# NF4 weight chunks worked out in turned layout, with block maxima from a second, natural copy

## The reference

```
x = x + attention(layernorm(x), ctx, ctx, mask; Wq, Wk, Wv, Wo)   # 32 query heads, 8 key/value heads of 128
x = x + ffn(layernorm(x); w1, w2, w3)

attention: q, k with rotary embedding; logits * 0.0884, 30*tanh(./30), masked softmax, times v, times Wo
ffn:       (silu(x @ dq(w1).T) * (x @ dq(w2).T)) @ dq(w3).T       # w1, w2: 1376 x 512, w3: 512 x 1376
dq(w):     flat = w.reshape(-1, 64); absmax = max|flat| per block of 64
           idx = searchsorted(bounds, flat / absmax); dq = NF4_CODE[idx] * absmax   # 16 levels, 15 bounds
```

## Time and profile before

| | |
|---|---|
| median of 3 runs | 800.41 us |
| profiled execution | 800.16 us |
| its span in the profile | 798.3 us |
| VectorE busy | 661.7 us, 83% of the span |
| ScalarE busy | 547.4 us, 69% |
| GpSimd busy | 367.3 us, 46% |
| moved by DMA | 87.56 MB, 110 GB/s on average |

### The profile page before, as it was taken

The page is one execution under the profiler, slowest core; times in us unless marked ns, Lnnn a source line. Parts: engine busy times, 40 slices in busy tenths (PEclk is TensorE's granted clock), DMA queues, the critical chain, the costliest instruction groups (busy, mean ns, idle before and its releaser), DMA issues.

```text
span 798.3 us, 10879 instructions
## 1 busy us (share of the span) xinstructions
PE 789.0 (99%) x3810; PEld 635.9 (80%) x3810; DVE 661.7 (83%) x741; ACT 547.4 (69%) x859; POOL 367.3 (46%) x210
## 2 busy tenths in 40 slices
PE   8999999999999999999999999999999999999998
PEld 6777887878887788878888888888778888888876
DVE  6897755898999999898988889899574999999913
ACT  6467737787877868678787788786643877868510
POOL 4773265446637457366465365473100534435010
PEclk9999999999999999999999999999999999999999
DMA  9636456333432433425235335231401031412022
GB/s 335 199 129 201 131 155 169 110 99 93 139 107 77 154 97 112 129 71 171 79 84 152 92 93 165 80 103 47 136 14 40 27 126 54 124 28 76 14 69 106
DMA packets 60981, 87.56 MB, mean 110 GB/s; under 512 B 6272, under 2 KB 29952, under 8 KB 60928
## 3 DMA queue, kind: packets, MB, share of 16 engines
q1 hardware_dynamic: 59744, 84.06, 35.7%
q10 hardware_dynamic: 1184, 2.82, 1.0%
HBM read 51.00 MB, written 19.07 MB: 88 GB/s over the span
## 4 chain that ended last, share of the span: by engine, by line
PE 85%; DVE 6%; issue 5%; ACT 2%; DMA 1%; POOL 0%; POOLq 0%; SPq 0%; DVEq 0%
PE bank L530 7%; PE prjs L514 7%; PE prjs L516 7%; PE bank L532 7%; PE bank L531 7%; PE prjs L515 7%; PE bank L590 7%; PE avp L618 6%; PE trp L503 4%; PE bank L496 3%; PE bank L498 3%; PE bank L497 3%; PE prjs L498 2%; PE prjs L496 2%; PE prjs L497 2%
## 5 line engine op out<-in xcount | busy, mean ns | idle before, releaser
L1294 POOL TENSOR_TENSOR qT<-cs_loop,sw 128x512 f32<-128x512 f32 x56 | 107.2, 1915 | 183.4 <-DMA sw<-cs_loop 176.1
L514 PE MATMUL prjs<-xh,wqh 128*128 128x512 f32 x256 | 123.3, 482 | 0.0
L530 PE MATMUL bank<-woh,ath 128*128 128x512 f32 x256 | 100.8, 394 | 1.0 <-DVE atl L1161 0.9
L516 PE MATMUL prjs<-xh,wql 128*128 128x512 f32 x256 | 100.2, 391 | 0.0
L532 PE MATMUL bank<-woh,atl 128*128 128x512 f32 x256 | 99.9, 390 | 0.0
L531 PE MATMUL bank<-wol,ath 128*128 128x512 f32 x256 | 99.7, 389 | 0.0
L862 ACT ACTIVATE ath<-trp 128x512 fp32r<-128x512 f32 x64 | 38.2, 596 | 89.5 <-PE trp L503 89.5
L515 PE MATMUL prjs<-xl,wqh 128*128 128x512 f32 x256 | 99.5, 389 | 0.0
L995 DVE TENSOR_TENSOR cs_loop<-prjs,csq 128x1024 f32<-128x1024 f32 x56 | 68.3, 1220 | 21.4 <-PE prjs L516 21.2
L987 DVE SCALAR_TENSOR_TENSOR nfv<-nfq,nfv 128x1408 f32<-128x1408 uint8 x42 | 79.1, 1883 | 0.2
L850 ACT ACTIVATE nrm<-avp,rs 128x128 f32<-128x128 f32 x256 | 72.6, 372 | 7.0 <-DVE rs L1148 6.7
(11 more groups left out here) (187 smaller groups left out, 1966.6 us busy)
## 6 DMA issues: line engine op xcount, KB each, us to landing
sw<-cs_loop SPq DMA_DIRECT2D x112, 128.0 KB, 2.3
stage<-wq_pieces SPq DMA_DIRECT2D x32, 256.0 KB, 2.9
stage<-wo_pieces SPq DMA_DIRECT2D x32, 256.0 KB, 3.1
stage<-dq_scratch SPq DMA_DIRECT2D x32, 256.0 KB, 3.2
ks_scratch<-qT SPq DMA_DIRECT2D x16, 256.0 KB, 3.1
vs_scratch<-vst SPq DMA_DIRECT2D x16, 256.0 KB, 3.5
kcur<-ks_scratch SPq DMA_DIRECT2D x16, 256.0 KB, 2.9
vcur<-vs_scratch SPq DMA_DIRECT2D x16, 256.0 KB, 3.4
```

The source lines that it names most:

```text
L514: nc.tensor.matmul(o, wqh[:, g, k, :], xh[:, k, cs], start=k == 0, stop=False)
L516: last = nc.tensor.matmul(o, wql[:, g, k, :], xh[:, k, cs], start=False, stop=k == KT - 1)
L530: nc.tensor.matmul(o, ah, wh[:, g, :], start=g == 0, stop=False)
L1294: nc.gpsimd.tensor_tensor(dst, products(ru, slot)[:, 0, :], sw[:, slot, :], ALU.add).then_inc(roped, 1)
```

## The change

The host now lays the chunks out turned: a partition holds a column of the contraction, so that the dequantised piece can be used as it lies, and the 64 values of a block lie in 64 (w1, w2) or 32 (w3, one of 4 parts) partitions. A second copy of the weights, `nf_natural`, in the old layout, is loaded as well, a chunk at a time (`nat_load`, buffer `nat`), for the maxima alone.

- `nf_top(k)` replaces `nf_prepare`: the same reduction and two small operations, on `nat`. For each k below 8 PE turns the 44 columns of maxima and reciprocals by one transpose (`turn_tops`), for w3 (k = 8 to 11 together) by two. ScalarE copies the rows out (`tops_rows`), SP stores them (`rows_store`: one transfer for k below 8, 32 small ones for w3).
- `scale_load(which, c)` loads them back, each row repeated over 64 or 32 partitions, into the one buffer `scl` (128 x 1408): two transfers for chunks 0 to 7, four for 8 to 11, before each normalising (which = 1) and each rescaling (which = 0).
- `nf_scale` replaces `nf_blocks`: both inputs are full 128 x 1408 tensors.
- All transposes of weights leave PE. `weight_hi`, `weight_lo`, `down_hi` and `w3_low` read `stage`, in SBUF; the loads of pieces wait for `wt_lo` in place of `wt_done`.
- The stream of items has all 12 maxima ahead: one per nine additions. 130 items (120 additions, 10 maxima) now lie in the loop, 34 in the hidden stage, 11 in the down stage. The maxima of chunk 0 move to VectorE's key unit 8 (turned on PE behind key unit 9), those of chunk 1 to value unit 10 (turned behind value unit 11).
- Chunks 0 to 7 are now those of w1 and w2, 8 to 11 those of w3. `nomask` and `keep` share the space of `eb`, and the scratch for dynamic DMA is set to 4096.

The diff, cut to its core:

```diff
+        SCALES = [(1, 0), (0, 0), (1, 1)] + ([x for c in range(2, 9) for x in ((1, c), (0, c - 1))]
+                                            + [(0, 8), (1, 9), (1, 10), (0, 9), (1, 11), (0, 10), (0, 11)])
+        ADDS = [(c, i) for c in range(1, 12) for i in range(15)]
+        STREAM = [x for n, add in enumerate(ADDS)
+                  for x in ([(n // 9 + 2, None)] if n % 9 == 0 and n < 90 else []) + [add]]
+        LOOP_ITEMS = STREAM.index((9, 0))
...
             if slot <= NSTEP:
-                return 122 * min(max(0, slot - 1), 55) // 55
+                return LOOP_ITEMS * min(max(0, slot - 1), 55) // 55
             if slot <= NSTEP + 2 * HT:
-                return 122 + 43 * min(max(slot - NSTEP - 2, 0), 20) // 20
-            return min(165 + max(0, 3 * (slot - NSTEP - 2 * HT) - 1), 16 * 11)
+                return LOOP_ITEMS + 34 * min(max(slot - NSTEP - 2, 0), 20) // 20
+            return min(LOOP_ITEMS + 34 + max(0, 3 * (slot - NSTEP - 2 * HT) - 1), len(STREAM))
...
+            def rows_store(k):
+                sp.wait_ge(rows_done, k + 1)
+                if k < 8:
+                    sp.dma_start(tops_d[k], rows[0:44, 0, :]).then_inc(rows_out, 16)
+                    return
+                for which in range(2):
+                    for part in range(4):
+                        to = tops3_d[which, part].rearrange("(n q a) r -> q a n r", q=2, a=2)
+                        for q, first in enumerate((part // 2, 21 + (part + 1) // 2)):
+                            for a in range(2):
+                                at = 44 * a + first
+                                sp.dma_start(to[q, a], rows[at:at + 21:2, which, :]).then_inc(rows_out, 16)
+            def scale_load(which, c):
...
+                    for half in range(2):
+                        at = 22 * which + 11 * half
+                        sp.dma_start(scl[64 * half:64 * half + 64, :],
+                                     tops_d[c, at:at + 11, :].rearrange("r h -> (r h)").partition_broadcast(64))\
+                            .then_inc(scale_in, 16)
...
+            def nf_transfers(slot):
+                for c in nf_norms(slot - 2):
+                    scale_load(0, c - 1)
+                for c in nf_finished(slot - 1):
+                    nf_store(c)
+                for c in nf_finished(slot - 2):
+                    if c < 7:
+                        nf_load(c + 2)
+                        scale_load(1, c + 2)
+                    if c == 7:
+                        scale_load(0, 8)
+                for k in nf_tops(slot - 2):
+                    if k < 8 or k == 11:
+                        rows_store(min(k, 8))
+                for k in nf_tops(slot - 1):
+                    if k < 11:
+                        nat_load(k + 1)
...
+            def turn_tops(k, j=0):
+                pe.wait_ge(nf_max, 3 * k + 3 if k < 8 else 36)
+                wait(pe, rows_done, k)
+                wait(pe, y_done, j)
...
-                    if last and b in (2, 3):
-                        weight_transposes(b - 2)
-                    if last and b == 5:
-                        weight_transposes(2)
+                    for k in tops_turned(j):
+                        turn_tops(k, j)
...
-                act.wait_ge(wt_done, n + 1)
+                if n == 0:
+                    act.wait_ge(roped, NK + NUNIT)
+                act.wait_ge(piece_in[n % 4], 16 * (STAGED + n // 4 + 1))
...
-                                     wt_bank(n)[:, :].rearrange("p (k h) -> p k h", k=KT), ACT.Copy).then_inc(wt_hi, 1)
+                                     stage[:, n % 4, :].rearrange("p (k h) -> p k h", k=KT), ACT.Copy).then_inc(wt_hi, 1)
...
-            def nf_blocks(buf, by):
-                blocks = buf[:, :].rearrange("p (b e) -> p b e", e=BLK)
-                return nc.gpsimd.tensor_tensor(blocks, blocks, by.rearrange("p (b o) -> p b o", o=1)
-                                               .to_broadcast([128, CH // BLK, BLK]), ALU.mult)
+            def nf_scale(buf):
+                return nc.gpsimd.tensor_tensor(buf[:, :], buf[:, :], scl[:, :], ALU.mult)
```

More of the change, by code:

```diff
@@ L74, in build @@
         nfp = sb("nfp", [128, 2, CH], u8)
-        nfm = sb("nfm", [128, 2, CH // BLK])
+        nat = sb("nat", [128, CH])
+        scl = sb("scl", [128, CH])
         nfg = sb("nfg", [128, CH // BLK])
-        nfr = sb("nfr", [128, CH // BLK])
+        tops = sb("tops", [128, 2, CH // BLK])
+        tops3 = sb("tops3", [128, 2, 4 * CH // BLK])
+        rows = sb("rows", [128, 2, 128])
         stage = sb("stage", [128, 4, 512])
@@ new lines, in scale_load @@
+            def scale_load(which, c):
+                if which == 0:
+                    if c in (8, 11):
+                        sp.wait_ge(nf_scaled, c)
+                    else:
+                        sp.wait_ge(nf_norm, c + 2 if c > 0 else 1)
+                else:
+                    wait(sp, nf_norm, c)
+                    wait(sp, nf_scaled, c if c in (1, 9) else c - 1)
+                if c < 8:
+                    sp.wait_ge(rows_out, 16 * (c + 1))
+                    for half in range(2):
[4 more added lines that the diff above has]
+                    return
+                sp.wait_ge(rows_out, 16 * 8 + 16 * 32)
+                for part in range(4):
+                    units = tops3_d[which, part, 11 * (c - 8):11 * (c - 7), :]
+                    sp.dma_start(scl[32 * part:32 * part + 32, :],
+                                 units.rearrange("u r -> (u r)").partition_broadcast(32)).then_inc(scale_in, 16)
@@ L543, in first_transposes @@
                 transpose4(trp, lambda k: nrm[:, i % 2, k * 128:(k + 1) * 128]).then_inc(xt_done, 1)
+            def turn_tops(k, j=0):
+                pe.wait_ge(nf_max, 3 * k + 3 if k < 8 else 36)
+                wait(pe, rows_done, k)
+                wait(pe, y_done, j)
+                out = tops_bank(k, j)
+                if k < 8:
+                    last = nc.tensor.transpose(out[0:44, 0:128], tops[:, :, :].rearrange("p w b -> p (w b)"), tab[:, 2, :])
+                else:
+                    for w in range(2):
+                        last = nc.tensor.transpose(out[0:88, w * 128:w * 128 + 128], tops3[:, w, :], tab[:, 2, :])
+                last.then_inc(nf_turned, 1)
             pe.wait_ge(consts, 2)
@@ L1378, in head @@
                         query_rope(j + AHEAD)
+                    if last and b == 3:
+                        nf_normalise(9)
                     if last and b in (2, 4, 6):
```

254 lines of the change are left out of this document (132 added, 122 removed).

## The result

The changed kernel takes 829.56 us (828.17 to 831.02 in 4 runs), the kernel before, run beside it, 800.48 us: 1.0363 times as long, interval 1.0343 to 1.0382. It is 29.1 us slower; the prediction said 8.0 us faster and at most 801. The profiled execution took 830.14 us with a span of 828.0 us.

The account below looks back on a forecast made before the run. PE, busy for 99% of the span, was taken to bound the kernel. The terms -15.3 + 1.5 + 2.1 - 0.6 + 3.0 + 0.5 + 0.8 = -8.0 us gave 792.4 us, range 786 to 801.

Parts of the forecast that it names:

- rival 3: SP's queue, blocked by 32 small stores of w3's maxima for 15.4 us: 0 to 5 us, 796 us; chance 0.13.
- Removed: Weight transposes leave PE: 22 groups at 0.46 us and 11 at 0.47 us, -15.3 us.
- Turnings: Nine turnings of maxima added on PE, 0.17 us each, +1.5 us.
- Start: Key projections: PE waits for first maxima, +2.1 us; chunk 1's maxima leave the place ahead of attention, -0.6 us.
- Loop: Attention loop: more VectorE items and longer GpSimd scalings make PE wait, +3.0 us, bounds 0 and 12.
- the carrying of lateness from slot to slot: Attention loop: averages, with five slots having both three additions and a longer scaling, give 3 us of waiting.
- End of attention: SP issues four scale transfers before the first four weight pieces, delaying them: +0.5 us, bounds 0 and 3.
- The gain is whole: Hidden stage: VectorE loses five additions and three maxima, keeps up with the shorter period, so no gain is lost.
- Tail: Down stage: tile 8 can start at 40.0 us, PE would be there at 38.1, so +0.8 us.
- Rival 2: Scale loads, repeating DRAM rows over partitions, take 16 us and come late: 829 us; chance 0.05.
- Rival 4: Hidden stage held by VectorE, its 20 low parts losing 0.92 us each: about 4 us, 796 us; chance 0.08.
- Rival 1: Attention loop bound by VectorE, each of 16 scalings costing it 2.4 us more: 806 us; chance 0.12, half mild.

Follow-up runs that it names:

- the four edits: Changed kernel with w3's maxima stored in two steps, hidden stage's first pieces earlier, chunk 10's store behind w3's first pieces, first maxima turned later: 805.03 us.
- pieces of the hidden stage earlier: Changed kernel with the hidden stage's first four weight pieces issued one token earlier, ahead of chunk 8's store: 823.68 us.
- turning back at unit 9: The four edits with scalings on VectorE, a table-laid stream, w3's maxima transfers four to a token, but first maxima turned behind key unit 9: 798.79 us.
- maxima in two steps: Changed kernel with w3's maxima stored by one transfer, then ordered by 16 device-memory transfers behind the next two tokens, replacing 32 stores: 820.47 us.
- chunk 10's store later: Changed kernel with chunk 10's store and the last load of scales put behind w3's first four pieces on SP's queue: 820.73 us.

## Why the prediction was wrong

The step that failed is the treatment of SP's queue. What it issues, or waits for, ahead of weight pieces was priced at 0.5 us at the end of attention, at nothing at the entry of the down stage, and was kept out of the sum for the 32 stores (rival 3). Taken out one by one these three cost 5.9, 8.8 and 9.1 us. The loop's term was mis-sized as well, 3.0 us for some 9.

- **Removed, -15.3: right.** Periods of 10.88 and 4.76 us as forecast. With the scaling left out on both sides, where nobody is late, the two stages are 13.4 us shorter from first to last matmul, and three of the 33 groups (1.4 us) stood ahead of them.
- **Turnings, +1.5: right, as far as one profile of each kernel tells.** With the scaling left out on both sides the loop with its seven turnings is 1.0 us longer, 0.15 each against 0.17.
- **Start, +2.1 and -0.6.** The wait is right to 0.25 us (2.35, for `tops`). The -0.6 did not come: the wait for `eb` is still there (0.7 us), and the one for chunk 1's maxima (0.6) came on top. Token 0 is 5.5 us late: 1.7 us more for the lower clock behind the wait, and 0.7 for `vst`. The cover named for the new loads, "asked for several units early", did not ask who stands behind them on SP's queue; a weight piece did when the maxima were turned later.
- **Loop, +3.0 (bounds 0 and 12).** Mechanism right, size off: 6.7 to token 44 in the changed kernel, 10.0 where the stalls are gone. Of the two prices named, the full operand's was right (3.2 us against an estimate of 3.5), and it costs VectorE what it adds, as taken. What failed is the carrying of lateness from slot to slot with averages: two thirds of the scalings' longer holds (7.4 of 11 us) reached TensorE, not those in the five slots with three additions alone.
- **Rival 3, SP's burst, 0 to 5 us: mis-sized.** An issue took 0.79 us and not 0.48, and the argument followed only the half-swaps and the products. What was hit first was the weight piece next in the queue, through ScalarE. Measured -9.1 us when taken out, and 18.6 us when put into the kernel before.
- **End of attention, +0.5 (0 to 3): failed.** It counted the four transfers ahead of the pieces, and not that the store of chunk 8 ahead of them waits for a scaling on GpSimd. Measured 5.9.
- **Entry of the down stage: not in the sum at all.** "The gain is whole" looked at VectorE's load. The diff moved chunk 10's store ahead of w3's pieces on SP. Measured 8.8.
- **Tail, +0.8:** too small. With the four edits tile 8 starts 41.5 us into the down stage (forecast 40.0; 43.1 before): TensorE waits 1.4 us for `hf` at tile 1, and is late at tiles 6 and 8, where three additions and a low part of VectorE's (5.8 us) stand between two tiles. In all the stage gained 2.1 us, not 4.4.
- **The clock: not in the sum.** Each long wait was priced at its own length. The stretches at the lower clock added some 2 us to each.
- **Rival 2, late scale loads:** no. 352 KB landed in a median 5.4 us and 176 KB in 4.7. GpSimd did wait for scales five times, 4.0 us at most, but creep and stalls have other causes. That the time measured is the 829 us of this rival is chance. **Rival 4:** no; the hidden stage kept TensorE's period. **Rival 1** named the right engine for the creep, but by itself that left the kernel at 805, not at 829.

Two thirds of the gap of 37.2 us to the forecast (829.6 less 792.4) are the four stalls (24.5 us with all edits). The rest, by the ledger of the kernel with the four edits: 5.7 us of creep beyond the terms for loop and turnings, 2.8 at the start, 2.3 in the down stage, where VectorE sets the pace, and some 2 at the end of attention and in the hidden stage.

## What to carry to other kernels

In this kernel the queue that issues in program order was on the critical path wherever something that waits, or a burst of small transfers, stood ahead of what a busy engine needed next. So for each moved or added entry write down the next three entries behind it and who needs them when. A wait of TensorE of a few us can cost more than its length: here 4.4 to 9.6 us of waiting were each followed by 3 to 5 us near 1.2 GHz. And a layout that needs a second full operand was not free for VectorE, although GpSimd did the work.

## What was not expected of the hardware

- GpSimd's multiplication of 128 x 1408 values took 2.54 us alone when the second operand was broadcast or was the first one itself, and 3.2 us when it was another buffer (with `scl` in the changed kernel, with `xh` in the kernel before).
- VectorE's addition and GpSimd's work on two operands in SBUF took turns: 4.47 us beside a scaling, 2.69 beside a low part of 1.28, 1.62 alone.
- The same wait of 2.3 us for the first maxima was followed by 3.7 us at a clock of 0.54 in the profile of the changed kernel, by such a stretch in two more (pieces of the hidden stage earlier; turning back at unit 9), and by full clock in two others (maxima in two steps; chunk 10's store later). Here is that stretch in the kernel with maxima in two steps:

```profile
37.80:41.40 3.60, 3.60 (x16) 2.92 (x17) 2.56 (x5) 0.38 (x1) 1.29 (x1) 1.00 0.28 106
```

- An issue on SP's queue took 0.79 us for a store of 11 partitions from SBUF and 0.61 us for one of twice the bytes within device memory (8 in 4.85 us).
